# Routing in pairs, step-zero masks inside the last attention chunk, and low parts by ScalarE with accumulating transfers

## The chip, the cores and the metric

One core of one Trainium2 chip runs one program. The metric is device time in microseconds of one execution, the median of three. Before the change it is 358.88 us (358.85 to 359.8).

## What is computed

The input is x, 16 x 128 tokens of width 128, and a context of the same shape. Four residual layers follow; three start with a layer norm. The fourth is a routed feed-forward with two iterations, and its first lines are the router. From the reference, cut:

```python
x = x + _L0_xattn_ref(_layernorm(x), ctx, ctx, ...)
x = x + _L0_ffn_ref(_layernorm(x), ...)
x = x + _L1_xattn_ref(_layernorm(x), ctx, ctx, ...)
x = x + _L1_ffn_ref(_layernorm(x), ...)

# _L1_ffn_ref
logits = _gelu(xf @ w_r1 + b_r1) @ w_r2 + b_r2
top_p, top_i = jax.lax.top_k(softmax(logits), 2)       # of 8 experts
for _ in range(2):
    ctx = concat([integrated, v])
    shared_ctrl = _gelu(ctx @ w_s1 + b_s1) @ w_s2 + b_s2
    hidden = _gelu(einsum(ctx_e, expert_w1[flat_idx]) + b1)
    ctrl = einsum(hidden, expert_w2[flat_idx]) + b2     # alpha, beta, gate
    x_r, v_r = _inl(ctrl, x_e, v_e, mu)                 # softplus, sigmoid, combined by top_p
    halt = sigmoid(_gelu(x_next @ w_h1 + b_h1) @ w_h2 + b_h2)
    refined = _gelu(x_next @ w_f1 + b_f1) @ w_f2 + b_f2
    integrated = integrated + halt * refined * integration_weight
```

## The kernel before

The 2048 tokens are cut into four chunks of 512, each of four blocks of 128. The program of every engine is written out by hand; engines meet only at counted semaphores, and each executes its own list in order.

After the weights are composed comes a loop over slots t (0 to 5). In slot t the first feed-forward of chunk t, the attention of chunk t-1, the layer norm and router of chunk t-2 ("rt") and the routing of chunk t-3 are interleaved. A layer norm is `ln_tok` (TensorE turns tokens, L1276), `ln_stats` and `ln_scale` (VectorE, L788 to L803) with the power -1/2 by GpSimd between them (L359), and `ln_zt` (TensorE turns back, L1297). `busy` multiplies without using the result; the table `FILL` and slot 4 place 9 such matmuls ahead of the attention norm of chunk 2, 2 and 14 ahead of the router norms of chunks 2 and 3, and 7 ahead of an expansion. `route(c)` (L847 to L863) is a chain of 14 small VectorE operations that finds the two experts of the tokens; `expand(c)` and `expand_weights(c)` (L1371, L1383, eight small transposes each) spread expert numbers and factors over the partitions, and ScalarE evicts them (L452, L458); `weigh` computes the factors and `slot_masks` the bias masks.

The fourth layer is a loop over eight steps s: chunks 0 to 3 in iteration one (s 0 to 3) and again in iteration two (s 4 to 7). TensorE in step s does `hidden(s+1)` (five tiles of three or, in iteration two, six matmuls, into two PSUM banks in turn, so that tile 2 waits until ScalarE has evicted tile 0), then the parts `controls(s, BETA)`, ALPHA (iteration two alone) and GATE. All these are float32r products in three pieces, high*high, low*high and high*low. ScalarE applies softplus or tanh to a part (`squashed`) and gelu to hidden tiles (L482, L484). VectorE makes the masked copies: `kept(s, j)` for tiles j = 1 to 3 (L897, into the two buffers hm), then in `lower(s, j)` their high part (L913, a cast) and their low part (L915, a subtraction of what the cast kept):

```python
dve.tensor_copy(out[:, 0, i, :], hm[j % 2]).then_inc(sem("hhi"), 1)
dve.wait_ge(sem("hhi"), (HT - 1) * s + j)
dve.tensor_tensor(out[:, 1, i, :], hm[j % 2], out[:, 0, i, :].bitcast(F), ALU.subtract)\
    .then_inc(sem("hlo"), 1)
```

`stepped(s)` combines the parts on VectorE (L1109 and on), and `refine_a`, `halt_a`, `refine_b` with `refine1`, `halt1`, `refine2` are the halt and refinement of the step before. GpSimd issues four accumulating transfers xi onto xT (L365).

## Time and profile before

| | |
|---|---|
| median of the runs | 358.88 us |
| the profiled execution's own time | 360.02 us |
| its span, first to last instruction | 358.2 us |
| TensorE matmul busy | 327.9 us (92%) |
| VectorE busy | 284.2 us (79%) |
| ScalarE busy | 196.2 us (55%) |
| GpSimd busy | 21.1 us (6%) |
| mean granted TensorE clock | 0.981 |

The times and the rows below come from one profiled execution. "Idle before" is time in which an engine waited, with what ended it. "PEclk" is the granted TensorE clock as a share of full speed, 2.4 GHz; 0.50 is 1.2 GHz. Starts are in us from the span's start.

### The profile page before, as it was taken

Reading aid. Unit: us, or ns where it says so; the run is one execution under the profiler, and the core shown is the slowest. Engines: PE = TensorE matmul, PEld = TensorE weight load, DVE = VectorE, ACT = ScalarE, POOL = GpSimd, SP = SyncE. Lnnn points to the kernel's source line nnn. Section 1 sums busy time; section 2 is a strip of 40 time slices with the busy share of each in tenths; the row PEclk is TensorE's granted clock in tenths of the full one; section 3 lists DMA queues with packets and bytes.
Section 4 is the critical chain, followed back from the end, with each engine's and each line's share of the span. In section 5 each row is a group of like instructions: output and inputs, shape, how many; then the busy total and the mean of one; then the engine's idle time right before and its main releaser. Section 6 shows DMA issues by size and latency. Waiting matters only on the chain.

```text
span 358.2 us, 4385 instructions
## 1 busy us (share of the span) xinstructions
PE 327.9 (92%) x1513; PEld 231.5 (65%) x1521; DVE 284.2 (79%) x598; ACT 196.2 (55%) x309; POOL 21.1 (6%) x24
## 2 busy tenths in 40 slices
PE   4989999899888889599798999999999999999996
PEld 4754787445454557367476677777777777777663
DVE  0556767655768777979997999999997997999694
ACT  2500025385637285186876686775855846734744
POOL 0040020202010112000000100000000000000000
PEclk9989999999999999789899999999999999999999
DMA  7999920000000000000000010100100100000001
...
DMA packets 11445, 18.92 MB, mean 53 GB/s; under 512 B 416, under 2 KB 8864, under 8 KB 10144
## 3 DMA queue, kind: packets, MB, share of 16 engines
...
q0 software_dynamic: 576, 1.05, 1.7%
...
HBM read 16.55 MB, written 1.05 MB: 49 GB/s over the span
## 4 chain that ended last, share of the span: by engine, by line
PE 70%; DVE 19%; issue 4%; ACT 3%; POOL 3%; DMA 2%; SPq 0%; DVEq 0%; ACTq 0%; POOLq 0%
PE ps L1200 65%; DVE zz L803 4%; POOL lrs L359 3%; DVE lst L788 2%; DMA ctxT<-in_ctxT 2%; PE ps L1297 1%; PE ps L1383 1%; PE ps L1276 1%; DVE lmv L791 1%; DVE st L688 1%; ACT hid L484 1%; PE ps L1371 1%; DVE a L704 1%; DVE lve L793 1%; DVE ctxT L1090 0%
## 5 line engine op out<-in xcount | busy, mean ns | idle before, releaser
L1200 PE MATMUL ps<-hm_odd,ew_hi 128*128 128x512 f32 (+1 forms) x164 | 52.3, 421 | 0.0
L1200 PE MATMUL ps<-hm_even,ew_hi 128*128 128x512 f32 (+1 forms) x160 | 49.7, 414 | 0.0
L1200 PEld LDWEIGHTS ps<-hm_odd,ew_hi 128*128 128x128 f32 (+1 forms) x164 | 29.1, 191 | 6.5 <-issue 0.5
L1200 PEld LDWEIGHTS ps<-hm_even,ew_hi 128*128 128x128 f32 (+1 forms) x160 | 27.5, 188 | 5.2
L1200 PE MATMUL ps<-hm_odd,ew_lo 128*128 128x512 f32 (+1 forms) x80 | 28.8, 397 | 0.0
L1200 PE MATMUL ps<-hm_even,ew_lo 128*128 128x512 f32 (+1 forms) x80 | 28.0, 390 | 0.0
L484 ACT ACTIVATE hid<-ps,pB 128x512 f32<-128x512 f32 x32 | 21.7, 687 | 10.4 <-PE ps L1200 9.7
L1200 PE MATMUL ps<-x_hi,w1x_hi 128*128 128x512 f32 x40 | 20.1, 503 | 5.7 <-ACT hid L484 3.9
L803 DVE TENSOR_SCALAR zz<-ps,lmv,lrs 128x128 f32<-128x128 f32 x48 | 16.4, 405 | 7.7 <-POOL lrs L359 7.5
L897 DVE SCALAR_TENSOR_TENSOR ring<-ring,pB,hid 128x1024 f32<-128x1024 bf16 x16 | 20.5, 1283 | 0.9
L788 DVE BATCH_NORM_STATS2 lst<-ps 128x6 f32<-128x128 f32 x48 | 10.7, 285 | 11.9 <-PE ps L1276 11.8
L1200 PE MATMUL ps<-zz,pB 128*128 128x512 f32 (+3 forms) x52 | 19.5, 503 | 0.5 <-DVE zz L1133 0.5
L359 POOL TENSOR_TENSOR lrs<-lve,mhalf 128x4 f32<-128x4 f32 x12 | 13.1, 1089 | 107.2 <-DVE lve L793 107.2
L1200 PE MATMUL ps<-ring,a 128*128 128x512 f32 x32 | 16.0, 652 | 1.0 <-DVE a L704 1.0
L1200 PE MATMUL ps<-x_lo,w1x_hi 128*128 128x512 f32 x40 | 16.9, 423 | 0.0
L1200 PE MATMUL ps<-x_hi,w1x_lo 128*128 128x512 f32 x40 | 16.7, 417 | 0.0
L1200 PEld LDWEIGHTS ps<-hm_odd,ew_lo 128*128 128x128 f32 (+1 forms) x80 | 14.2, 191 | 3.0
L1200 PE MATMUL ps<-zz,wz 128*128 128x512 f32 x32 | 15.7, 596 | 0.0
L1200 PEld LDWEIGHTS ps<-hm_even,ew_lo 128*128 128x128 f32 (+1 forms) x80 | 13.7, 188 | 2.7
L595 ACT ACTIVATE kv<-ps 128x1024 f32<-128x1024 f32 x15 | 15.3, 1017 | 0.0
L1200 PEld LDWEIGHTS ps<-b,ring 128*128 128x128 f32 x128 | 14.7, 192 | 0.6 <-issue 0.5
L1200 PE MATMUL ps<-b,ring 128*128 128x128 f32 x128 | 15.0, 276 | 0.0
...
## 6 DMA issues: line engine op xcount, KB each, us to landing
...
```

What stands on the lines that cost most here:

```text
L359: pool.tensor_tensor(lrs[:, n % 2, :], lve[:, n % 2, :], mhalf[:, 0:BPC], ALU.pow)\
L484: act.activation(hid[:, j, :], hid_bank(s, j), ACT.Gelu, bias=W("eb1", j, j + 1)).then_inc(sem("hid"), 1)
L595: act.activation(out[:, 1:3], group_ps(n)[:, 1:3], f, scale=scale).then_inc(sem("squash"), 1)
L688: dve.bn_stats(st[:, b, :], xtok[:, b, :]).then_inc(sem("st"), 1)
L704: dve.tensor_tensor(a1[:, :, :], a1[:, :, :], wcol[:, 0, :].unsqueeze(2).to_broadcast([128, KC, D]), ALU.mult).then_inc(sem("a1s"), 1)
L788: dve.bn_stats(lst[:, n % 2, j, :], t[:, j * D:(j + 1) * D]).then_inc(sem("lst"), 1)
L791: dve.bn_aggr(lmv[:, n % 2, j, :], lst[:, n % 2, j, :]).then_inc(sem("lmv"), 1)
L793: dve.tensor_scalar(lve[:, n % 2, :], lmv[:, n % 2, :, 1], EPS, None, ALU.add)\
L803: dve.tensor_scalar(ztok[:, n % 2, j, :], t[:, j * D:(j + 1) * D], lmv[:, n % 2, j, 0:1], lrs[:, n % 2, j:j + 1], ALU.subtract, ALU.mult)\
L897: dve.scalar_tensor_tensor(hm[j % 2], idx[:, c, :, :], W("tile_expert", j, j + 1), hid[:, j, :].unsqueeze(1).to_broadcast([128, 2, CH]), A ...
L1200: return pe.matmul(out, lhsT, rhs, start=start, stop=stop)
L1276: last = pe.transpose(bank[n % 2][:, j * 128:(j + 1) * 128], xT[:, t * 128:(t + 1) * 128], ident)
```

## The change

Routing runs for two chunks at a time: `logits(c)` copies each chunk's logits alone, and `route(c)` and `weigh(c)` work on eight blocks. In slots 2 and 3 no routing, expansion or weighing is left between the norms. The slots end after t = 3; the rest of chunk 3's attention, the router norms of chunks 2 and 3 and the hidden tiles and masks of step 0 follow in a list of their own, in which the hidden tiles come in the order 1, 2, 0, 3 and shared. The 23 `busy` matmuls ahead of the router norms and the expansion are gone. `controls(0, BETA)` now stands ahead of `router2(3)` and `hidden(1)`, with the last router norm inside it; expansions and weights of later chunks move into steps 0, 1 and 2.

For tiles 2 and 3 of every step VectorE no longer subtracts. ScalarE writes the negated high part (`negative_high`; the target is float32r, so the copy rounds) into the low half of the masks, and GpSimd adds the unrounded masks by an accumulating transfer of 128 x 1024 (`low_part`), 16 in all. In a BETA part the high products of tiles 2 and 3 now come ahead of all their low products. Three PSUM banks swap roles with the other three, which changes no count.

```diff
-            for n in range(3 * NCH):
+            def power(n):
                 pool.wait_ge(sem("lve"), n + 1)
                 pool.tensor_tensor(lrs[:, n % 2, :], lve[:, n % 2, :], mhalf[:, 0:BPC], ALU.pow)\
...
-            for s in range(NCH):
+            def low_part(s, j):
+                pool.wait_ge(sem("nhi"), 2 * s + j - 1)
+                if s >= 1:
+                    pool.wait_ge(sem(f"hlo_{j}"), 16 * s)
+                pool.dma_start(low_of(s, j), hm[j % 2], accum_op=ALU.add).then_inc(sem(f"hlo_{j}"), 16)
...
+            for n in range(3 * NCH - 1):
+                power(n)
+            low_part(0, 2)
+            power(3 * NCH - 1)
+            low_part(0, 3)
+            for s in range(1, STEPS):
+                if 3 <= s < NCH + 3:
+                    residual(s - 3)
+                low_part(s, 2)
+                low_part(s, 3)
...
+            def negative_high(s, j):
+                act.wait_ge(sem("hm"), (HT - 1) * s + j)
+                act.activation(low_of(s, j), hm[j % 2], ACT.Copy, scale=-1.0).then_inc(sem("nhi"), 1)
+            z_att(3)
+            q_evac(3)
+            expand_evac(0, 2, 3)
+            exps(3)
+            second_exp(0)
+            hidden_gelus(0, (1, 2))
+            ln_evac("rt", 2, xi[:, ck(2)])
+            hidden_gelus(0, (0, 3))
+            r1_gelu(2)
+            hidden_gelus(0, (HT,))
+            negative_high(0, 2)
+            expand_evac(1, 3, 2)
+            ln_evac("rt", 3, xi[:, ck(3)])
+            negative_high(0, 3)
+            r1_gelu(3)
...
             for s in range(STEPS):
+                if s == 0:
+                    squashed(0, BETA)
+                    hidden_gelus(1)
+                    state_high(2)
+                    second_exp(2)
+                    weights_evac(0, 7, 6)
+                    expand_evac(2, 7, 6)
+                    negative_high(1, 2)
+                    negative_high(1, 3)
+                    squashed(0, GATE)
+                    continue
                 if s + 1 < STEPS:
                     hidden_gelus(s + 1)
-                if s == 0:
-                    second_exp(NCH - 2, 2)
                 if s == 1:
-                    weights_evac(NCH - 1, 7, 6)
+                    expand_evac(3, 7, 6)
+                    weights_evac(1, 7, 6)
                 if s >= 2:
                     refine2(s - 2)
+                if s == 2:
+                    weights_evac(2, 7, 6)
+                    weights_evac(3, 7, 6)
                 if s + 2 < STEPS:
                     state_high(s + 2)
                 squashed(s, BETA)
-                if s >= 1:
+                refine1(s - 1)
+                halt1(s - 1)
+                if s + 1 < STEPS:
+                    negative_high(s + 1, 2)
+                    negative_high(s + 1, 3)
                 squashed(s, parts(s)[1])
...
+            def logits(c):
+                t = slice(c * BPC, (c + 1) * BPC)
+                dve.wait_ge(sem("lg_ps"), c + 1)
+                dve.tensor_copy(lg[:, t, :], router_bank(c)[:, 0:BPC * E].rearrange("p (b e) -> p b e", b=BPC))\
+                    .then_inc(sem("lg"), 1)
...
+                t = slice(c * BPC, (c + 2) * BPC)
+                eq = eq_2[:, :, :]
+                iota = W("iota").unsqueeze(1).to_broadcast([128, 2 * BPC, E])
...
+            def high(s, j):
+                dve.wait_ge(sem("hm"), (HT - 1) * s + j)
+                dve.tensor_copy(high_of(s, j), hm[j % 2]).then_inc(sem("hhi"), 1)
...
                 kept(s, 2)
+                if s == 2:
+                    weigh(2)
                 if next_state:
                     state_split(s + 1)
                 lower(s, 0)
+                high(s, 1)
                 lower(s, 1)
                 kept(s, 3)
-                lower(s, 2)
+                high(s, 2)
                 shared_halves(s)
-                lower(s, 3)
+                high(s, 3)
+                if s <= 2:
+                    slot_masks(s + 1)
...
+            route(0)
+            att_add(2)
+            ln_stats("rt", 2)
+            att_max(3)
+            slot_masks(0)
+            ln_scale("rt", 2)
+            kept(0, 1)
+            att_norm(3)
+            high(0, 1)
+            lower(0, 1)
             kept(0, 2)
-            lower(0, 1)
+            att_pt(3)
+            high(0, 2)
+            att_add(3)
+            logits(2)
+            slot_masks(1)
+            ln_stats("rt", 3)
             kept(0, 3)
+            lower(0, 0)
+            ln_scale("rt", 3)
+            high(0, 3)
+            shared_halves(0)
             state_split(1)
-            lower(0, 2)
-            shared_halves(0)
-            lower(0, 3)
-            route(NCH - 1)
+            weigh(0)
+            logits(3)
+            route(2)
             dve.wait_ge(sem("consts"), 4)
...
-            FILL = {("att", 0): 5, ("att", 1): 4, ("att", 2): 9, ("rt", 2): 2, ("rt", 3): 14}
+            FILL = {("att", 0): 5, ("att", 1): 4, ("att", 2): 9}
...
+            att_v(2)
+            ln_zt("att", 3)
+            q_proj(3)
+            pe.wait_ge(sem("fh"), FT * NCH)
+            expand(0, 2, 3)
+            ln_tok("rt", 2, "x3")
+            scores(3)
+            hidden(0, (1, 2))
+            ln_zt("rt", 2)
+            hidden(0, (0, 3))
+            probs_t(3)
+            router1(2)
+            hidden(0, (HT,))
+            router2(2)
+            att_v(3)
+            pe.wait_ge(sem("hid"), HT)
+            pe.wait_ge(sem("hsu"), 1)
+            expand(1, 3, 2)
+            ln_tok("rt", 3, "x3")
             pe.wait_ge(sem("bp"), 1)
...
+                def high(i):
+                    j, k = TILES[i]
+                    pe.wait_ge(sem("hhi"), (HT - 1) * s + j)
+                    mm((lo, hi)[k], weights(ew2_hi, j), m[:, 0, i, :], start=rows_last and j == 1, stop=False)
+                    mm((lo, hi)[k], weights(ew2_lo, j), m[:, 0, i, :], start=False, stop=False)
+                def low(i):
+                    j, k = TILES[i]
+                    if j == 1:
+                        pe.wait_ge(sem("hlo"), 1 if s == 0 else 2 * s + 2)
+                    else:
+                        pe.wait_ge(sem(f"hlo_{j}"), 16 * (s + 1))
+                    last = mm((lo, hi)[k], weights(ew2_hi, j), m[:, 1, i, :], start=False,
+                              stop=not rows_last and j == HT - 1)
+                    if n == LAST and j == HT - 1:
+                        last.then_inc(sem("stream_ps"), 1)
+                    return last
...
                 for i in (1, 3, 5, 2, 4, 6) if n == LAST else range(1, NT):
-                    j, k = TILES[i]
-                    if i == 4 and between:
-                        between()
-                    pe.wait_ge(sem("hlo"), HT * s + j + 1)
-                    out = hi if k else lo
-                    mm(out, weights(ew2_hi, j), m[:, 0, i, :], start=rows_last and j == 1, stop=False)
-                    mm(out, weights(ew2_lo, j), m[:, 0, i, :], start=False, stop=False)
-                    last = mm(out, weights(ew2_hi, j), m[:, 1, i, :], start=False,
-                              stop=not rows_last and j == HT - 1)
-                    if n == LAST and j == HT - 1:
-                        last.then_inc(sem("stream_ps"), 1)
+                    if i in between:
+                        between[i]()
+                    high(i)
+                    if not rows_last or i < 3:
+                        last = low(i)
+                if rows_last:
+                    for i in range(3, NT):
+                        low(i)
                 if rows_last:
                     shared(True)
...
+                if s == 0:
+                    def routed():
+                        ln_zt("rt", 3)
+                        router1(3)
+                    def weights_0():
+                        pe.wait_ge(sem("hid"), 2 * HT)
+                        pe.wait_ge(sem("hsu"), 2)
+                        expand_weights(0, 7, 6)
+                    def expand_2():
+                        pe.wait_ge(sem("cb"), 2)
+                        expand(2, 7, 6)
+                    controls(0, BETA, between={5: routed})
+                    router2(3)
+                    hidden(1)
+                    controls(0, GATE, between={2: weights_0, 4: expand_2})
+                    continue
+                def expand_3():
+                    pe.wait_ge(sem("hid"), 3 * HT)
+                    pe.wait_ge(sem("hsu"), 3)
+                    expand(3, 7, 6)
+                def weights_1():
+                    pe.wait_ge(sem("idx"), 2 * NCH)
+                    expand_weights(1, 7, 6)
+                def weights_2():
+                    pe.wait_ge(sem("rr"), 1)
+                    pe.wait_ge(sem("th"), 1)
+                    expand_weights(2, 7, 6)
+                def weights_3():
+                    pe.wait_ge(sem("cb"), 6)
+                    expand_weights(3, 7, 6)
                 if s + 1 < STEPS:
                     hidden(s + 1)
                 if s >= 2:
                     refine_b(s - 2)
```

How it moves instructions at the three places that matter:

VectorE in slot 3, from the statistics of chunk 3's attention norm. Before (L788, L793 statistics, L847 to L863 routing, L803 scaling):

```order
180 L793 TENSOR_SCALAR lve<-lmv 128x4 [waits lmv]
181 L847 COPY lg<-ps 128x32 [waits lg_ps]
182 L850 TENSOR_REDUCE rt<-lg 128x4 [waits lg]
183 L851 TENSOR_TENSOR eq<-lg,rt 128x32 [waits dve_chain]
184 L852 TENSOR_TENSOR eq<-eq,pB 128x32 [waits dve_chain]
```

Now:

```order
156 L846 TENSOR_SCALAR lve<-lmv 128x4 [waits lmv]
157 L856 TENSOR_SCALAR zz<-ps,lmv,lrs 128x128 [waits zt_ps,lrs]
158 L856 TENSOR_SCALAR zz<-ps,lmv,lrs 128x128 x3
159 L895 COPY lg<-ps 128x32 [waits lg_ps]
160 L908 TENSOR_REDUCE rt<-lg 128x8 [waits lg]
161 L909 TENSOR_TENSOR eq<-lg,rt 128x64 [waits dve_chain]
```

The scaling stands ahead of the routing, which handles two chunks in one chain.

TensorE in the part BETA of step 0, tiles 1 and 2, before (each hlo is counted up by a subtraction on VectorE):

```order
220 L1200 MATMUL ps<-hm_even,ew_hi 128x512 [waits hlo]
221 L1200 MATMUL ps<-hm_even,ew_lo 128x512
222 L1200 MATMUL ps<-hm_even,ew_hi 128x512
223 L1200 MATMUL ps<-hm_even,ew_hi 128x512 [waits hlo]
224 L1200 MATMUL ps<-hm_even,ew_lo 128x512
225 L1200 MATMUL ps<-hm_even,ew_hi 128x512
```

Now, from the turning back of chunk 3's router norm (pA,zz) and `router1(3)` (xi,pB) in the middle of that part to its end; hlo_2 and hlo_3 are the semaphores of the transfers:

```order
190 L1365 MATMUL ps<-pA,zz 128x128 [waits ztok,z]
191 L1365 MATMUL ps<-pA,zz 128x128 x3
192 L1268 MATMUL ps<-xi,pB 32x512 [waits lg,x2,z]
193 L1268 MATMUL ps<-hm_even,ew_hi 128x512 [waits hhi]
194 L1268 MATMUL ps<-hm_even,ew_lo 128x512
195 L1268 MATMUL ps<-hm_even,ew_hi 128x512 [waits hhi]
196 L1268 MATMUL ps<-hm_even,ew_lo 128x512
197 L1268 MATMUL ps<-hm_even,ew_hi 128x512 [waits hlo_2] x2
198 L1268 MATMUL ps<-hm_even,ew_hi 128x512 [waits hlo_3] x2
199 L1268 MATMUL ps<-hsh,ws_hi 128x512 [waits hsl]
```

The last router norm and its transfer now lie inside a part, whose last products wait for tile 3's transfer.

ScalarE at the end of step 1, before (L565 and L566 are `halt1`, L594 and L595 the squashed GATE, L482 the next hidden tile 0):

```order
115 L565 ACTIVATE zz<-ps,pB 128x512 [waits h1_ps]
116 L566 ACTIVATE h1s<-ps,pB 128x512
117 L594 ACTIVATE kv<-ps,bs2h 128x512 [waits part_ps,xn]
118 L595 ACTIVATE kv<-ps 128x1024
119 L482 ACTIVATE hm_odd<-ps,pB 128x512 [waits part_ps,hlo,hid_ps]
```

Now:

```order
117 L608 ACTIVATE h1s<-ps,pB 128x512
118 L565 ACTIVATE hm_even<-wz 128x1024 [waits hm]
119 L565 ACTIVATE hm_even<-ring 128x1024 [waits hm]
120 L636 ACTIVATE kv<-ps,bs2h 128x512 [waits part_ps,xn]
121 L637 ACTIVATE kv<-ps 128x1024
122 L519 ACTIVATE hm_odd<-ps,pB 128x512 [waits part_ps,hlo,hid_ps]
```

The two negated copies stand between `halt1` and the squashed GATE.

## Rows read from the trace of the kernel before

**Rows 1.** Stretches, all engines: us, busy (count) per engine, PEclk, DMA share, GB/s

```profile
99.71:122.43 22.72, 19.17 (x100) 12.65 (x99) 17.26 (x74) 10.65 (x23) 2.06 (x3) 1.00 0.00 1
122.43:156.78 34.35, 26.72 (x125) 18.65 (x128) 27.49 (x84) 18.01 (x34) 2.99 (x2) 0.90 0.00 0
156.78:197.63 40.85, 36.84 (x173) 27.28 (x173) 36.77 (x50) 30.50 (x43) 0.00 (x0) 0.96 0.01 1
197.63:331.72 134.09, 134.09 (x599) 98.82 (x603) 125.81 (x135) 84.12 (x114) 3.65 (x4) 1.00 0.05 10
```

**Rows 2.** Timeline of TensorE, waits of 1 us and more, and the late one

```profile
150.31 0.99 PE L1200 MATMUL ps<-x_hi,w1x_hi 128*128 128x512 f32 x1 [1.60 <-DVE x_lo L929]
...
174.50 0.50 PE L1200 MATMUL ps<-x_hi,w1x_hi 128*128 128x512 f32 x1 [2.65 <-ACT hid L484]
...
195.89 0.50 PE L1200 MATMUL ps<-x_hi,w1x_hi 128*128 128x512 f32 x1 [1.28 <-ACT hid L484]
...
332.60 0.47 PE L1200 MATMUL ps<-xn_hi,wf_hi 128*128 128x512 f32 x1 [0.87 <-issue]
```

**Rows 3.** Stretches around two falls of the granted clock (PEclk third from the end)

```profile
150.31:155.00 4.69, 4.57 (x10) 3.08 (x11) 4.49 (x8) 1.92 (x3) 0.00 (x0) 0.50 0.00 0
172.40:175.80 3.40, 1.30 (x6) 1.05 (x6) 3.33 (x3) 2.91 (x5) 0.00 (x0) 0.99 0.00 0
175.90:179.10 3.20, 3.20 (x9) 2.28 (x8) 3.13 (x4) 2.15 (x4) 0.00 (x0) 0.50 0.01 3
```

**Rows 4.** Timeline of VectorE: one of each kind of its work

```profile
98.80 0.19 DVE L850 TENSOR_REDUCE rt<-lg 128x4 f32<-128x32 f32 x1
...
116.76 0.89 DVE L788 BATCH_NORM_STATS2 lst<-ps 128x6 f32<-128x128 f32 x4 [0.95 <-PE ps L1276]
...
118.05 0.18 DVE L847 COPY lg<-ps 128x32 f32<-128x32 f32 x1
...
120.92 1.37 DVE L803 TENSOR_SCALAR zz<-ps,lmv,lrs 128x128 f32<-128x128 f32 x4
122.20 0.74 DVE L835 SCALAR_TENSOR_TENSOR xT<-ps,bvo,xT 128x512 f32<-128x512 f32 x1
...
144.29 1.28 DVE L897 SCALAR_TENSOR_TENSOR wz<-ring,pB,hid 128x1024 f32<-128x1024 bf16 x1
145.49 0.69 DVE L913 CAST hm_even<-ring 128x1024 fp32r<-128x1024 f32 x1
146.21 1.23 DVE L915 TENSOR_TENSOR hm_even<-ring,hm_even 128x1024 fp32r<-128x1024 f32 x1
```

**Rows 5.** Groups of the small transposes, 99 to 200 us: busy, mean ns | idle before

```profile
L1371 PE MATMUL ps<-pA,tif 128*128 128x128 f32 x32 | 4.3, 276 | 0.9 <-DVE tif L862 0.9
L1383 PE MATMUL ps<-pA,cf 128*128 128x128 f32 x32 | 4.2, 275 | 0.0
```

**Rows 6.** Timeline of ScalarE: a copy, a table load, two ends of step, hidden tile 0

```profile
159.67 0.62 ACT L547 ACTIVATE x_hi<-xi 128x512 fp32r<-128x512 f32 x1
...
160.92 1.28 ACT L594 ACT_TABLE_LOAD   x1
...
193.08 0.69 ACT L594 ACTIVATE kv<-ps,bs2h 128x512 f32<-128x512 f32 x1 [0.90 <-PE ps L1200]
193.66 1.02 ACT L595 ACTIVATE kv<-ps 128x1024 f32<-128x1024 f32 x1
...
214.06 0.69 ACT L594 ACTIVATE kv<-ps,bs2h 128x512 f32<-128x512 f32 x1 [0.88 <-PE ps L1200]
214.65 1.02 ACT L595 ACTIVATE kv<-ps 128x1024 f32<-128x1024 f32 x1
...
216.21 1.50 ACT L484 ACTIVATE hid<-ps,pB 128x512 f32<-128x512 f32 x2
```

**Rows 7.** Timeline of TensorE, tile 2 of `hidden(4)`, next to rows 6

```profile
216.95 0.50 PE L1200 MATMUL ps<-x_hi,w1x_hi 128*128 128x512 f32 x1
```

**Rows 8.** The accumulating transfers: L365's landing, and the queue (packets, MB, share)

```profile
DMA to landing us min/median/max: 3.3/3.4/3.7
...
q0 software_dynamic: 576, 1.05, 1.7%
```

More of the change, by code:

```diff
@@ L513, in _ @@
                     q_evac(t - 1)
-                if f and t:
+                if t:
                     gelus(t, (3,))
@@ L1003, in _ @@
             weights_low()
-            for t in range(SLOTS):
-                f, a, q, x = (0 <= t - i < NCH for i in range(4))
+            for t in range(NCH):
+                a, q = t >= 1, t >= 2
                 if t + 2 < NCH:
@@ L1011, in _ @@
                     ln_scale("ffn", t + 2)
-                if x and not f:
-                    slot_masks(t - 3)
                 if q:
                     ln_stats("rt", t - 2)
-                if t == SLOTS - 1:
-                    kept(0, 1)
-                    lower(0, 0)
                 if a:
```

270 lines of the change are left out of this document (106 added, 164 removed).

## Prediction

> **What bounds the kernel now.** I read the stretches first. From 197.63 to 331.72 us TensorE is busy for the whole 134.09 us, at full clock, while VectorE is busy for 125.81 and ScalarE for 84.12 [rows 1]. So in steps 2 to 7 only TensorE's own work counts, one matmul per 0.22 us (134.09 / 599). Ahead of that it is not full: 19.17 of 22.72, 26.72 of 34.35 and 36.84 of 40.85 us, part of it at a lowered clock. The timeline says why [rows 2]: it waits 1.60 us for VectorE's x_lo, and 2.65 and 1.28 us for ScalarE's hidden tile 0. The 0.87 us at 332.60 is again a wait for VectorE (the second input split of step 6), although the row says issue. The reader should see that the change can gain only ahead of 197.63 us and at that late wait, and lose anywhere.
>
> **The sum** goes along the path that leads to the first step without waits, against the profiled execution's own span of 358.2 us (its own time is 360.02, 1.1 above the median 358.88; I add the difference to the median). "Lead" is how much earlier a thing happens than before.
>
> *To the last attention norm.* In slot 3 the routing of 14 small operations stands between statistics and scaling: from 118.05 to 120.92 us, 2.9 us [rows 4]. It moves behind; the power on GpSimd, about 1 us, stays. That gives some 1.7 us, and the same in the slot before gives 1.3, since TensorE's nine filling matmuls then end last. One expansion and one set of weights leave the slot, 1.07 us each (4.3 us for four) [rows 5]. Lead 1.7 + 1.3 + 2.1 = 5.1: the scaled tokens of chunk 3's attention are complete at 117.2 instead of 122.3.
>
> *To the last router norm.* Now VectorE has the whole list to itself, and TensorE waits for it; the 23 fills that go had filled such waits (5.2 us), so they give nothing, but they had held the clock up. By kinds [rows 4]: two statistics 2.8 with their aggregates, two scalings 2.6, three masked copies at 1.2 make 3.6, two casts 1.4, low parts 1.25 and 0.65, two additions 1.4, two pairs of bias masks 1.4, attention maximum, norm and copy 2.3, logits 0.2. The paired routing is 14 operations at 0.22 us on twice the columns. Its bounds are 2.9 (no more than one chunk now) and 5.7 (twice that); I take 3.1, as the 0.19 us of these tiny tiles [rows 4] is mostly fixed. Sum 20.7. Waits between them: 0.8 for token transposes, 1.7 for ScalarE (four exponentials, a table load of 1.28 [rows 6], one gelu), 0.5 and 0.6 for the attention output and the expansion. 24.2 in all: the last router norm is scaled at 141.4; before it was ready at 144.4, ahead of the row at 144.29 [rows 4]. The lead is down to 3.
>
> *Into the first part.* BETA of step 0 has begun at 135.6 by the same addition, but needs tile 3's low part: transposes 0.5, eviction 0.6, the negated copy, then the transfer. The copy is bounded by two of the 0.62 us copies and by the 1.02 us of a 1024-wide eviction [rows 6]; I take 1.0. The transfer moves 512 KB; the trace shows 256 KB landing in 3.3 to 3.7 us [rows 8]. Bounds are 3.4 (size costs nothing) and 6.8 (all of it scales). The queue's share, 1.7% of 16 engines' span, is 97 us for 576 packets, so 0.17 each; 128 over 16 engines take 1.35 us, doubling adds that: 4.75, which I take. The Trainium skill, DMA: Bandwidth & Descriptors, section Anatomy of one DMA, gives 2.0 us plus bytes over 436e3 instead, an estimate of 3.2 us; by that the sum would end 1.5 us lower. The rows, with 3.4 for half the size, speak for more. So 143.5 + 4.75 = 148.2.
> The rest of the part is 1.85 us. TensorE will have waited about 3.3 us twice; before, after a stretch with 1.30 of 3.40 us busy, 3.2 us at half clock followed [rows 3], so I add 1.5: 151.6. ScalarE then squashes (1.6), loads gelu (1.3) and makes tile 0 (1.3) before TensorE's last three tiles of `hidden(1)` (2.2): 158.0. GATE with 2.0 us of transposes takes 7.6 and ends at 165.6. Before, that was 174.50 - 2.65 - 1.75 = 170.1 [rows 2].
>
> *Steps 1 to 3.* In step 0 ScalarE has x_hi, a load, weights and expansion (to 164.3), two negated copies, GATE (1.6), a load, and tile 0: `hidden(2)` goes on at 170.5 instead of 174.5. Lead 4.0. BETA of step 1 holds one expansion more; I count 0.6 of its 1.0, as a half-clock stretch of before [rows 3] becomes shorter: 3.4. At the end of a step ScalarE used to wait 0.90 and 0.88 us for TensorE ahead of GATE [rows 6]. Now two copies, 2.0 us, stand there, so GATE is 1.1 late, and with it the next tile 0, for which TensorE already waits at 195.89 [rows 2]: 2.3. Step 2 gets the weights of chunks 2 and 3, which used to be done by then, in the full stretch: -2.1, left 0.2. At the ends of steps 2 and 3 the two copies cost again. Tile 2 of `hidden(4)` starts at 216.95 [rows 7], when the gelus that began at 216.21 have just made tile 0 [rows 6], so nearly nothing hides them: 2 x 1.05 = 2.1. In steps 4 to 6 the copies stand ahead of ALPHA and the GATE part hides them; if it didn't, three more such microseconds would come. VectorE has 2.5 us less per step (two times 1.23 [rows 4]), so the late wait of 0.87 goes; ScalarE's chain is next there. At the end of step 1 TensorE waits 2.5 us, which may lower the clock: 0.8.
> In all 3.4 - 1.1 - 2.1 - 2.1 + 0.9 - 0.8 = -1.8. **Forecast: 358.9 + 1.8 = 360.7 us**, own range 358.7 to 362.9 (transfer 3.4 or 6.8, clock lowered or not). About 0.3% (1.1 us) is what a measurement of this kernel can tell from no change.
>
> **Rivals.**
> *The lead survives (0.22).* For it: VectorE's list is shorter by 1.23 us twice a step, and every TensorE wait ahead of 197.63 has VectorE or ScalarE as its end. If the low part lands in 3.4 us (1.35 less) and the clock stays up (1.5 and 0.8 less), the sum is 1.8 - 3.7 = -1.9: 357.0 us. It decides whether TensorE reaches step 2 more than 4.5 us ahead, which pays for the late weights and the copies. Against: without the fills TensorE is emptier than in the stretch that lost its clock [rows 3].
> *Late low parts (0.17).* One GpSimd queue carries 20 transfers instead of four. If a 512 KB one needs 6.8 us or more, TensorE stands 2 us longer in BETA of step 0, and at 8 us 3.3: 362.7 to 364. In later steps the masks are made 10 us ahead, so only this one counts. The four landings, 3.3 to 3.7 us beside running VectorE work [rows 8], speak against it. The Trainium skill, SBUF — State Buffer, section on the two separate sides, says that a VectorE copy between SBUF tiles in its fast mode keeps GpSimd from writing descriptors, so such a transfer seems blocked. Here each transfer of tile 3 is issued next to a cast of 0.69 us [rows 4]; as a mechanism of this kernel that adds up to 0.7 us and gives 361.4, inside my own range.
> *VectorE was the pace (0.02).* It is 94% busy in the full stretch [rows 1]. If it set the step, 2.46 us in each of six steps would go: 344 us. TensorE's 134.09 us without a gap speak against it.
> *It does nothing on balance (0.04):* the moved work was hidden anyway, 358.9.
>
> **Chances.** Forecast 0.55, of which 0.21 lies within 0.3%; the lead survives 0.22, mostly over 0.3% faster; late low parts 0.17; the rest 0.06. Faster 0.21, same 0.25, slower 0.54. The range for 8 in 10 reaches to the first rival and to the second: 356.7 to 364.7.
>
> **What would show it.** The scaled tokens of chunk 3's attention near 117; TensorE waiting 3 us and more in BETA of step 0 for a transfer issued near 143.5; landings of 4.5 to 5 us; `hidden(3)` tile 2 near 193.5 after a wait of 2.5 us; new waits of about 1 us ahead of tile 2 in `hidden(4)` and `hidden(5)`; none for x_lo near 332. The prediction is wrong if TensorE has no waits at the ends of steps 2 and 3, if the negated copies take well under 1 us, or if the full stretch starts more than 4 us earlier.

## The result, and the profile after

| | before | changed |
|---|---|---|
| median of the runs | 359.34 us (358.85 to 359.83, 4 runs) | 365.35 us (363.7 to 366.37, 4 runs) |
| ratio, 95% interval | | 1.0163 (1.0119 to 1.0207) |
| span of the profiled execution | 358.2 us | 364.2 us |
| mean granted TensorE clock | 0.981 | 0.963 |
| TensorE, VectorE busy | 327.9, 284.2 us | 328.4, 259.6 us |
| ScalarE, GpSimd busy | 196.2, 21.1 us | 210.6, 35.2 us |

The changed kernel is 6.0 us slower. The forecast had the sign, with 1.8 us, but 365.35 lies above the range's end of 364.7. VectorE was relieved by 24.6 us, and the kernel still became longer. The changed kernel's profile is that of its slowest run, 366.37 us.

The same four stretches as in [rows 1], changed kernel:

```profile
99.71:122.43 22.72, 19.10 (x86) 11.64 (x85) 14.89 (x55) 9.72 (x20) 2.43 (x3) 0.93 0.00 1
122.43:156.78 34.35, 25.20 (x110) 16.03 (x108) 20.04 (x55) 17.21 (x32) 4.98 (x4) 0.80 0.16 31
156.78:197.63 40.85, 33.58 (x166) 24.50 (x165) 32.78 (x58) 34.19 (x49) 3.77 (x4) 1.00 0.18 34
197.63:331.72 134.09, 132.11 (x589) 97.54 (x590) 110.41 (x120) 93.39 (x128) 12.04 (x14) 0.99 0.29 55
```

The second stretch stands out: the granted clock is 0.80 where it was 0.90, although TensorE has less to do. VectorE is busy for only 20.04 of its 34.35 us, so its own work doesn't fill the stretch; what it waits for is read below.

TensorE's timeline of the changed kernel, its waits and what ran behind them ([rows 2, 7] for before):

```profile
117.72 0.63 PE L1365 MATMUL ps<-pA,zz 128*128 128x128 f32 x4 [1.72 <-DVE zz L856]
119.09 1.87 PE L1268 MATMUL ps<-wz,pB 128*128 128x512 f32 x2 [0.75 <-ACT wz L435]
...
127.41 0.63 PE L1365 MATMUL ps<-pA,zz 128*128 128x128 f32 x4 [1.90 <-DVE zz L856]
...
133.71 1.92 PE L1268 MATMUL ps<-xi,pB 128*32 128x512 f32 x2
...
146.48 0.94 PE L1365 MATMUL ps<-pA,zz 128*128 128x128 f32 x4 [3.70 <-DVE zz L856]
148.11 1.91 PE L1268 MATMUL ps<-xi,pB 128*32 128x512 f32 x2 [0.69 <-ACT xi L435]
...
153.93 0.73 PE L1268 MATMUL ps<-hm_even,ew_hi 128*128 128x512 f32 x2 [1.05 <-DMA hm_even<-ring]
...
172.43 0.38 PE L1268 MATMUL ps<-xtok,others 128*128 128x512 bf16 x1 [1.75 <-DVE xtok L943]
...
175.33 0.50 PE L1268 MATMUL ps<-x_hi,w1x_hi 128*128 128x512 f32 x1 [1.13 <-ACT hid L521]
...
198.04 0.80 PE L1268 MATMUL ps<-x_hi,w1x_hi 128*128 128x512 f32 x1 [2.17 <-ACT hid L521]
...
223.13 0.51 PE L1268 MATMUL ps<-x_hi,w1x_hi 128*128 128x512 f32 x1 [0.80 <-ACT hid L521]
...
246.90 0.50 PE L1268 MATMUL ps<-x_hi,w1x_hi 128*128 128x512 f32 x1 [0.77 <-ACT hid L521]
```

The clock can be read from the second number, the duration. The projection at 119.09 and the router products at 133.71 and 148.11 take 1.87 to 1.92 us; at the full clock they take 1.04 to 1.12, as kernel e1 below shows. The clock has fallen three times by 150 us, each time behind waits. The wait at 172.43 is new, for chunk 2's slot masks; those at 223.13 and 246.90, ahead of tile 2 of `hidden(4)` and `hidden(5)`, are new too and were forecast (about 1 us each). VectorE's waits for TensorE behind the first and the second low stretch, and the queue and landings (min, median, max) of the transfers:

```profile
123.25 0.89 DVE L841 BATCH_NORM_STATS2 lst<-ps 128x6 f32<-128x128 f32 x4 [1.79 <-PE ps L1344]
...
139.02 0.75 DVE L888 SCALAR_TENSOR_TENSOR xT<-ps,bvo,xT 128x512 f32<-128x512 f32 x1 [3.76 <-PE ps L1268]
...
DMA to landing us min/median/max: 4.6/4.8/6.5
...
q0 software_dynamic: 2880, 9.44, 13.9%
```

### The profile page after: what moved, and what is told of

Same layout as the page of the kernel before. It is cut to its first block, busy times and chain, and to the rows that moved or that the text cites. A ratio compares the mean times of both kernels' runs of the same rounds, so it can differ in the third digit from the quotient of the medians.

```text
span 364.2 us, 4348 instructions
## 1 busy us (share of the span) xinstructions
PE 328.4 (90%) x1498; PEld 228.5 (63%) x1498; DVE 259.6 (71%) x546; ACT 210.6 (58%) x324; POOL 35.2 (10%) x40
## 3 DMA queue, kind: packets, MB, share of 16 engines
HBM read 16.55 MB, written 1.05 MB: 48 GB/s over the span
## 4 chain that ended last, share of the span: by engine, by line
PE 66%; DVE 13%; ACT 8%; issue 5%; POOL 3%; DMA 3%; SPq 0%; DVEq 0%; ACTq 0%; POOLq 0%
PE ps L1268 61%; DVE zz L856 3%; POOL lrs L378 3%; DVE lst L841 2%; PE ps L1365 2%; DMA ctxT<-in_ctxT 2%; ACT hid L521 1%; DMA hm_even<-ring 1%; PE ps L1344 1%; PE ps L1439 1%; PE ps L1449 1%; DVE st L741 1%; DVE lmv L844 1%; ACT zz L607 1%; ACT kv L636 1%
## 5 line engine op out<-in xcount | busy, mean ns | idle before, releaser
L1268 PE MATMUL ps<-hm_even,ew_hi 128*128 128x512 f32 (+1 forms) x160 | 51.8, 425 | 1.1 <-DMA hm_even<-ring 1.1
L959 DVE SCALAR_TENSOR_TENSOR ring<-ring,pB,hid 128x1024 f32<-128x1024 bf16 x16 | 20.5, 1283 | 3.3 <-ACT hid L521 1.6
L1268 PE MATMUL ps<-ring,a 128*128 128x512 f32 x32 | 17.3, 696 | 1.0 <-DVE a L757 1.0
L1365 PE MATMUL ps<-pA,zz 128*128 128x128 f32 x48 | 7.9, 288 | 11.2 <-DVE zz L856 11.2
L1268 PEld LDWEIGHTS ps<-x_hi,w1x_hi 128*128 128x128 f32 x40 | 8.1, 203 | 15.0 <-ACT hid L521 12.4
L1365 PEld LDWEIGHTS ps<-pA,zz 128*128 128x128 f32 x48 | 5.3, 143 | 17.1 <-issue 15.0
```

What stands on the lines that cost most here:

```text
L959: dve.scalar_tensor_tensor(hm[j % 2], idx[:, c, :, :], W("tile_expert", j, j + 1), hid[:, j, :].unsqueeze(1).to_broadcast([128, 2, CH]), A ...
L1268: return pe.matmul(out, lhsT, rhs, start=start, stop=stop)
L1365: last = pe.transpose(bank[6][:, j * 128:(j + 1) * 128], ztok[:, n % 2, j, :], ident)
```

## The experiments

Executions differ by up to 1.6 us already at the first norm's transposes (47.17 to 48.76 us), up to which all these kernels do the same work. The table counts from there, in us. Each row is one profiled execution, whose own time is given ("profiled"); it isn't always near the median, so differences below 1 or 2 us between ends are not to be read from it. The kernel before was run beside each of these kernels, with medians of 359.25 to 359.48. Below, brackets behind a time hold the lowest and highest run, those behind a ratio its 95% interval.

| kernel | chunk 3's last norm, transposes | hidden(2), first gelu | hidden(3), first gelu | end | profiled | median us |
|---|---|---|---|---|---|---|
| before | 96.6 | 125.3 | 146.7 | 310.4 | 360.02 | 359.3 |
| changed | 98.3 | 125.8 | 148.5 | 316.0 | 366.37 | 365.35 |
| e1: fills | 94.5 | 123.2 | 145.9 | 312.1 | 363.02 | 363.76 |
| e2: before without fills | 98.5 | 127.0 | 148.1 | 311.8 | 361.31 | 361.29 |
| e3: copies behind the gate | 98.2 | 127.4 | 152.3 | 322.9 | 373.62 | 372.56 |
| e4: all lows on VectorE | 97.2 | 127.6 | 150.2 | 315.8 | 365.49 | 365.78 |
| e11: step 0's lows on VectorE | 97.9 | 125.4 | 148.0 | 314.3 | 363.8 | 364.13 |
| e6: fills, masks, step 0's lows | 94.5 | 119.4 | 142.8 | 309.1 | 359.27 | 357.05 |
| e7: fills, masks, lows of steps 0 to 4 | 94.4 | 117.8 | 143.3 | 308.2 | 357.65 | 358.2 |
| e9: e7 and chunk 3's masks | 94.4 | 117.8 | 139.6 | 304.8 | 353.81 | 354.14 |
| e10: e9, all lows on VectorE | 94.4 | 117.8 | 139.6 | 305.5 | 354.53 | 355.42 |
| e12: e9 without fills | 98.2 | 125.6 | 147.4 | 312.3 | 362.83 | 362.38 |

**1. Fills back (e1).** `ew2_hi` products into a free bank, at three waits.

```diff
-            FILL = {("att", 0): 5, ("att", 1): 4, ("att", 2): 9}
+            FILL = {("att", 0): 5, ("att", 1): 4, ("att", 2): 9, ("att", 3): 7, ("rt", 2): 8, ("rt", 3): 14}
```

> The changed kernel with 29 filling matmuls put back into three waits of TensorE ahead of step 0: 7 ahead of the transposes of chunk 3's attention norm (1.72 us idle), 8 ahead of chunk 2's last norm (1.90 us) and 14 ahead of chunk 3's last norm (3.70 us); nothing else differs. Theory 1 (the forecast failed because TensorE ran at the lower clock in 119-122.5, 129-136 and 147-154 us, and that stretched the chain between VectorE and TensorE): the granted clock of 122-157 us rises from 0.80 to above 0.9, chunk 3's last norm is scaled at about 142 us in place of 144.97, step 0's Beta products end near 152 in place of 156, and the kernel takes 3 to 5 us less than the changed one's 365.35, so about 361. Theory 2 (the chain's length is set by VectorE, ScalarE and the transfer, and the lower clock only filled waits): under 1 us, so 364.5 to 366.

Measured: 363.76 us (362.58 to 364.51), ratio to before 1.0123 (1.0104 to 1.0142): 1.6 us less than the changed kernel. TensorE's timeline:

```profile
118.18 0.66 PE L1365 MATMUL ps<-pA,zz 128*128 128x128 f32 x4
119.59 1.12 PE L1268 MATMUL ps<-wz,pB 128*128 128x512 f32 x2 [0.75 <-ACT wz L435]
...
139.50 3.33 PE L1268 MATMUL ps<-ew_hi 128*128 128x512 f32 x14
143.25 0.66 PE L1365 MATMUL ps<-pA,zz 128*128 128x128 f32 x4 [0.42 <-DVE zz L856]
144.59 1.04 PE L1268 MATMUL ps<-xi,pB 128*32 128x512 f32 x2 [0.69 <-ACT xi L435]
...
150.41 0.98 PE L1268 MATMUL ps<-hm_even,ew_hi 128*128 128x512 f32 x2 [3.20 <-DMA hm_even<-ring]
151.20 0.63 PE L1268 MATMUL ps<-hsh,ws_hi 128*128 128x512 f32 x1
```

Its VectorE, at the two waits for TensorE that were shown for the changed kernel:

```profile
122.83 0.89 DVE L841 BATCH_NORM_STATS2 lst<-ps 128x6 f32<-128x128 f32 x4 [0.82 <-PE ps L1344]
...
135.87 0.75 DVE L888 SCALAR_TENSOR_TENSOR xT<-ps,bvo,xT 128x512 f32<-128x512 f32 x1 [1.03 <-PE ps L1268]
```

The clock stays up to 150 us (0.95 over 122 to 157 us, where the changed kernel had 0.80), and the last norm comes 3.8 us earlier (94.5 against 98.3). VectorE waits 0.82 us for the tokens in place of 1.79, and 1.03 us for the attention product in place of 3.76: 3.7 us together. At hidden(3) 2.6 us of it are left, and between the medians 1.6, though the intervals of the two kernels overlap. The rest is lost at the next limit: TensorE now waits 3.20 us for the transfer of tile 3's low part, and behind that wait the clock falls (0.63 us for one product, not 0.39). The expected size was wrong; the mechanism of theory 1 is there, with a second limit behind it.

**2. The kernel before without its 23 fills (e2).**

```diff
-            FILL = {("att", 0): 5, ("att", 1): 4, ("att", 2): 9, ("rt", 2): 2, ("rt", 3): 14}
+            FILL = {("att", 0): 5, ("att", 1): 4, ("att", 2): 9}
...
-                    busy(7 if t == SLOTS - 2 else 0, bank[2])
+                    busy(0, bank[2])
```

> The kernel before without its 23 filling matmuls in the two last slots (2 and 14 ahead of the last two norms, 7 ahead of an expansion). Theory 1 (these hold up the clock through the chain ahead of step 0): the stretch at 0.5 moves ahead of 147 us, the list is longer, and the kernel takes 2 to 4 us more than 359. Theory 2 (they only fill waits; the clock falls at 149.5 us with them anyway): within 1 us of 359.

Measured: 361.29 us (360.25 to 362.6), ratio 1.0060 (1.0039 to 1.0081). Stretches of the kernel before, then of this one:

```profile
143.00:150.00 7.00, 2.81 (x14) 1.57 (x14) 6.81 (x11) 1.28 (x2) 0.00 (x0) 0.89 0.00 0
```

```profile
143.00:150.00 7.00, 3.00 (x6) 0.90 (x6) 6.56 (x10) 0.64 (x2) 1.68 (x1) 0.64 0.00 0
```

The clock falls earlier, and the kernel takes 2.0 us more, at the lower end of theory 1's range. So dropping the fills with nothing else touched costs about two of the 6.0 us by which the changed kernel is slower.

**3. Negated copies behind the gate (e3).**

```diff
-                    negative_high(s + 1, 2)
-                    negative_high(s + 1, 3)
                 squashed(s, parts(s)[1])
+                if s + 1 < STEPS:
+                    negative_high(s + 1, 2)
+                    negative_high(s + 1, 3)
```

(and likewise in step 0)

> The changed kernel with ScalarE's two negated copies put behind the squashing of the step's last gate in steps 0 to 6, in place of ahead of it. Theory 1 (two copies of 0.94 us stand in the way of the squashing and of the next gelus at the ends of steps 1, 2 and 3, as the prediction has it at 1.1 and 1.05 each): 2.5 to 3.5 us less than the changed kernel, 362 to 363; the waits of TensorE at the next step's third hidden tile go back to those of before. Theory 2 (the copies then stand ahead of the next gelus and the low parts land too late for the next Beta products, so it is only moved): no change, 365, or slower.

Measured: 372.56 us (370.38 to 373.72), ratio 1.0366 (1.0340 to 1.0392): 7.2 us more than the changed kernel, a clear miss of theory 1. ScalarE at the end of step 1, first in the changed kernel, then in this one:

```profile
192.77 0.68 ACT L608 ACTIVATE h1s<-ps,pB 128x512 fp32r<-128x512 f32 x1
193.34 1.06 ACT L565 ACTIVATE hm_even<-wz 128x1024 fp32r<-128x1024 f32 x1
194.28 1.06 ACT L565 ACTIVATE hm_even<-ring 128x1024 fp32r<-128x1024 f32 x1
195.23 0.69 ACT L636 ACTIVATE kv<-ps,bs2h 128x512 f32<-128x512 f32 x1
...
196.71 0.70 ACT L519 ACTIVATE hm_odd<-ps,pB 128x512 fp32r<-128x512 f32 x1
```

```profile
195.96 0.68 ACT L608 ACTIVATE h1s<-ps,pB 128x512 fp32r<-128x512 f32 x1
197.53 0.69 ACT L636 ACTIVATE kv<-ps,bs2h 128x512 f32<-128x512 f32 x1 [0.89 <-PE ps L1268]
...
199.02 1.06 ACT L565 ACTIVATE hm_even<-wz 128x1024 fp32r<-128x1024 f32 x1
199.97 1.06 ACT L565 ACTIVATE hm_even<-ring 128x1024 fp32r<-128x1024 f32 x1
200.92 0.69 ACT L519 ACTIVATE hm_odd<-ps,pB 128x512 fp32r<-128x512 f32 x1
```

Ahead of the gate the copies stand partly in a wait of 0.89 us, so 1.9 us of copies cost about 1. Behind it they cost the whole 1.9 to the next gelus (from h1s to tile 0's first gelu 4.96 us, against 3.94). TensorE's wait at the third hidden tile is then 3.17 us in place of 2.17, with a half-clock stretch of over 4 us behind it. The place that the change chose was the better one.

**4. All low parts back on VectorE (e4).** `negative_high` and `low_part` do nothing, and in `high`:

```diff
+                if j >= 2:
+                    dve.wait_ge(sem("hhi"), (HT - 1) * s + j)
+                    dve.tensor_tensor(low_of(s, j), hm[j % 2], high_of(s, j).bitcast(F), ALU.subtract)\
+                        .then_inc(sem(f"hlo_{j}"), 16)
```

> The changed kernel with all low parts back on VectorE: no negated copies on ScalarE, no accumulating transfers; VectorE has two subtractions of 1.23 us more in each step and in the list ahead of step 0. Routing in pairs, the order of the list and the missing fills stay. Theory 1 (the prediction's: the copies cost 1.1 + 1.05 + 1.05 at ends of steps, the transfer's 4.6 us against 1.2 of a subtraction costs 2 to 3 ahead of step 0, the late low parts 0.9): 3 to 6 us less than the changed kernel, 359.5 to 362. Theory 2 (VectorE, which has two subtractions more ahead of the last norm and in each step, sets the pace): no better, 365 or more. If the fills alone explain the miss, this kernel still lies at or over 359.

Measured: 365.78 us (362.42 to 367.06), ratio 1.0164 (1.0128 to 1.0200): no better, the number of theory 2. In the trace the gain of theory 1 is there, `hidden(3)` to `hidden(4)` takes 22.96 us in place of 25.09 (23.82 in e1, with the clock up), but 1.7 us are lost ahead of that. This is TensorE's timeline:

```profile
173.61 0.99 PE L1268 MATMUL ps<-x_hi,w1x_hi 128*128 128x512 f32 x1 [4.10 <-DVE xtok L939]
```

The last operation of VectorE's list in a step is the pair of slot masks for the step after, which TensorE needs first. With two subtractions more ahead of it, the wait is 4.10 us, not 1.75. So it is less the pace of VectorE over a whole step than the place of the masks in its list. That led to the kernels e7 and e9.

**5. Slot masks early, with fills (e5).** In `hidden_masked`, besides the line of e1:

```diff
+                if s == 1:
+                    slot_masks(2)
                 high(s, 2)
                 shared_halves(s)
                 high(s, 3)
-                if s <= 2:
-                    slot_masks(s + 1)
+                if s == 2:
+                    slot_masks(3)
```

> The changed kernel with the 29 filling matmuls in three waits (363.76 us so) and with chunk 2's slot masks made before the cast of step 1's second tile, not after its last cast, so some 2 us earlier; TensorE waited 1.76 us for them ahead of the third step's hidden products. Theory 1 (that wait costs what it reads): 1.2 to 1.7 us less than 363.76. Theory 2 (ScalarE is still busy with the squashed gate and the gelu table load until the hidden products are there, and TensorE only meets it one tile later): within 0.4 us of 363.76, and TensorE's wait at the third hidden tile grows from 1.12 to above 2 us.

Measured: 363.99 us, ratio 1.0133 (1.0116 to 1.0149), so nothing against e1's 363.76: theory 2. e5 has no trace of its own that could be read. In e6, which has this edit and one more, the wait at the third hidden tile is 3.00 us at 169.09 in place of e1's 1.12; that fits the forecast growth, but isn't shown for e5 itself. The 1.75 us wait of the changed kernel is real in the trace and costs nothing by this run; there ScalarE loads its gelu table until 174.0, 1.6 us after TensorE's wait has ended.

**6. Step 0's low parts on VectorE, with fills and early masks (e6), and alone (e11).**

```diff
+                if j >= 2 and s < 1:
+                    dve.wait_ge(sem("hhi"), (HT - 1) * s + j)
+                    dve.tensor_tensor(low_of(s, j), hm[j % 2], high_of(s, j).bitcast(F), ALU.subtract)\
+                        .then_inc(sem(f"vlo_{j}"), 1)
```

(the negated copy and the transfer return early for `s < 1`)

> As the kernel with fills and early slot masks, and the low parts of step 0's tiles 2 and 3 by VectorE (two subtractions of 1.23 us) in place of negated copy and accumulating transfer; steps 1 to 7 keep the transfers. Theory 1 (with the clock restored, TensorE's 3.20 us wait for the transfer of tile 3's low part sets the end of step 0's Beta products): that wait goes, VectorE's list grows by up to 1.2 us ahead of chunk 3's last norm, and 2 to 2.8 us less, near 361.5. Theory 2 (VectorE's list is the pace, and the longer list takes back what the transfer gave): within 0.7 us of the same kernel with the transfers.

> The changed kernel with the low parts of step 0's tiles 2 and 3 by VectorE, and nothing else: no fills, masks where they were. With fills this edit took 6.9 us off together with the masks. Theory 1 (without the fills the clock falls and the late norm hides the transfer: TensorE waited only 1.05 us for it): 1 to 2 us less than 365.35, so the two repairs work only together. Theory 2 (the transfer's 4.6 us is a cost by itself): 4 to 6 us less, 359.5 to 361.5.

Measured: e6 357.05 us (356.54 to 359.27), ratio 0.9940 (0.9912 to 0.9969); e11 364.13 us (363.8 to 365.05), ratio 1.0144 (1.0125 to 1.0163). TensorE's timeline of e6, where e1 has its wait of 3.20 us:

```profile
142.86 0.66 PE L1378 MATMUL ps<-pA,zz 128*128 128x128 f32 x4 [0.30 <-DVE zz L860]
...
146.21 1.07 PE L1281 MATMUL ps<-hm_even,ew_hi 128*128 128x512 f32 x4
147.12 0.39 PE L1281 MATMUL ps<-hsh,ws_hi 128*128 128x512 f32 x1
```

Alone the edit gives 1.2 us by the medians, alone the fills give 1.6; together, with the masks, 8.3. The intervals of e11 and e1 overlap with that of the changed kernel, so each single gain may be anything from nothing to some 3 us; that their sum stays below 8.3 is beyond the noise. The masks were worth nothing in e5. In e6 they weren't taken out alone, but its trace leaves room: VectorE's last cast ends at 166.1, so masks made last would come 1.8 us after TensorE's start at 164.34, and ScalarE can't take tile 0 before 167.77 anyway. Each of the two costs had hidden the other: with late tokens the transfer was nearly covered (TensorE waited 1.05 us for it), and with the transfer the early tokens ran into a wait of 3.20 us, behind which the clock fell. In e6 two more subtractions on VectorE don't delay the last norm at all (94.5 in both).

**7. Low parts of steps 0 to 4 on VectorE (e7), chunk 3's masks early too (e9), all on VectorE (e10).** The limits `s < 1` become `s < 5` and `s < 8`; e9 and e10 have

```diff
-                high(s, 2)
-                shared_halves(s)
-                high(s, 3)
                 if s <= 2:
                     slot_masks(s + 1)
+                high(s, 2)
+                shared_halves(s)
+                high(s, 3)
```

> As the kernel before it, and the low parts of steps 0 to 4 by VectorE; only steps 5 to 7 keep the negated copies and transfers. Theory 1 (two copies of 0.94 us ahead of the squashed gate cost 0.9, 0.87 and 0.81 at the ends of steps 1, 2 and 3; in steps 4 to 7 TensorE has no waits, so they cost nothing there): 1.7 to 2.6 us less than with only step 0 on VectorE, near 359.3. Theory 2 (VectorE with 2.46 us more in each step gets late for the step's last products, as in the kernel before, and nothing is won): within 0.7 us.

> The kernel with 29 fills and the low parts of steps 0 to 4 on VectorE, and now chunk 3's slot masks too before the cast of step 2's second tile, some 5 us earlier; there TensorE waited 3.51 us for them ahead of hidden(3), and ScalarE 3.50 for TensorE. Theory 1 (this late pair of masks took the gain that the freed ScalarE had given): both waits go, ScalarE's gelus of hidden(3) start right behind the squashed gate, and 2.4 to 3.4 us less than 358.2, so 355 to 356. Theory 2 (VectorE's longer list delays the next step anyway): within 0.7 us of 358.2.

> As the kernel before it with all low parts on VectorE, so without negated copies and accumulating transfers in steps 5 to 7. Theory 1 (the transfers relieve VectorE near the end: from hidden(7)'s first gelu to the end it took 61.3 us with them and 62.2 without): 0.7 to 1.1 us more than the kernel before it. Theory 2 (TensorE is busy without a gap there, and who makes the low parts is nothing to it): the same within 0.3 us.

Measured: e7 358.2 us (357.03 to 360.33), ratio 0.9977 (0.9959 to 0.9995); e9 **354.14 us** (353.81 to 355.9), ratio **0.9865** (0.9845 to 0.9885); e10 355.42 us (354.53 to 356.88), ratio 0.9898 (0.9876 to 0.9920). TensorE at `hidden(3)`, e7 and then e9:

```profile
189.19 0.80 PE L1281 MATMUL ps<-x_hi,w1x_hi 128*128 128x512 f32 x1 [3.51 <-DVE xtok L947]
```

```profile
188.20 0.50 PE L1279 MATMUL ps<-x_hi,w1x_hi 128*128 128x512 f32 x1 [1.28 <-ACT hid L523]
```

ScalarE at the same place in e7, and TensorE near the end of e10 (e9 has no wait there):

```profile
190.88 0.69 ACT L521 ACTIVATE hm_odd<-ps,pB 128x512 fp32r<-128x512 f32 x1 [3.50 <-PE ps L1281]
```

```profile
327.07 0.47 PE L1279 MATMUL ps<-xn_hi,wf_hi 128*128 128x512 f32 x1 [0.86 <-issue]
```

e7 missed both ways: it was no faster than e6, but 1.1 us slower by the medians (the intervals overlap), and its longer list put the masks 3.51 us late. In e9 that wait is gone and 4.1 us with it, more than the row said, for the half-clock stretch behind it goes too. So the same kind of wait was worth nothing in e5 and 4.1 us here; what differs is ScalarE, which in e7 had nothing to do and waited 3.50 us for the hidden products. From e6 to e9 hidden(3) to hidden(4) falls from 23.84 to 23.14 us and hidden(4) to hidden(5) from 23.77 to 23.03: 0.7 each for two negated copies. And e10 against e9: without the transfers of steps 5 to 7 the late wait of the kernel before is back (0.86 us at 327.07), and from hidden(7)'s first gelu to the end it takes 62.18 us, not 61.38. So the transfers do help there, by 0.8 us in the traces and 1.3 between the medians.

**8. Ten more fills than e7, in three waits of 0.7 to 1.1 us (e8).** In `q_proj`, `hidden(0)` and `router1`:

```diff
+                if c == 3:
+                    busy(3, bank[5])
...
+                        if j == 0:
+                            pe.wait_ge(sem("x2"), NCH)
+                            pe.wait_ge(sem("lg"), 2)
+                            busy(4, bank[4])
...
+                if c == 3:
+                    busy(3, bank[1])
```

> As the kernel before it, with 10 more filling matmuls in three short waits of TensorE (3 while chunk 3's attention norm is evicted, 4 ahead of hidden tile 0, 3 while chunk 3's last norm is evicted). Theory 1 (short gaps one after the other bring the clock down too): the clock of 117 to 157 us is 1.00 throughout, and 0.5 to 1.5 us less. Theory 2 (only the three long waits mattered): the same time within 0.4 us.

Measured: 358.08 us (356.74 to 359.77), ratio 0.9974 (0.9955 to 0.9993); e7 was 358.2. Theory 2: with the three long waits filled, 122 to 157 us was at 1.00 already.

**9. The fastest kernel without the fills (e12).**

```diff
-            FILL = {("att", 0): 5, ("att", 1): 4, ("att", 2): 9, ("att", 3): 7, ("rt", 2): 8, ("rt", 3): 14}
+            FILL = {("att", 0): 5, ("att", 1): 4, ("att", 2): 9}
```

> The fastest kernel so far (354.14 us: fills, early slot masks, low parts of steps 0 to 4 on VectorE) with the 29 filling matmuls taken out again. Theory 1 (the fills are half of what the miss was: with the transfer gone from the list ahead of step 0, the clock is what is left there): the clock of 122 to 157 us falls to about 0.8, step 0's Beta products are evicted 3 to 5 us later, and 3 to 5 us more, 357 to 359. Theory 2 (the fills are worth no more than the 1.6 us that they gave the changed kernel, whatever else is there): 355.3 to 356.2.

Measured: 362.38 us (361.79 to 362.83), ratio 1.0084 (1.0070 to 1.0098): 8.2 us more than e9, beyond both theories; the mechanism is theory 1's, its size is double. Stretches of e9, then of e12:

```profile
129.00:136.00 7.00, 6.92 (x42) 5.02 (x43) 6.33 (x9) 5.13 (x9) 0.00 (x0) 1.00 0.01 2
...
143.00:150.00 7.00, 6.99 (x35) 4.71 (x35) 4.96 (x19) 4.96 (x6) 0.00 (x0) 1.00 0.00 0
150.00:157.00 7.00, 5.15 (x26) 3.37 (x26) 4.42 (x12) 6.12 (x10) 0.00 (x0) 1.00 0.00 0
157.00:164.00 7.00, 6.75 (x38) 5.19 (x35) 6.73 (x10) 4.76 (x9) 0.00 (x0) 1.00 0.01 2
```

```profile
129.00:136.00 7.00, 5.69 (x13) 2.58 (x14) 6.57 (x9) 3.31 (x6) 0.00 (x0) 0.57 0.00 0
...
143.00:150.00 7.00, 2.68 (x8) 0.71 (x6) 6.54 (x14) 0.60 (x1) 1.98 (x1) 0.79 0.00 0
150.00:157.00 7.00, 7.00 (x30) 5.25 (x31) 2.34 (x12) 3.98 (x5) 0.00 (x0) 0.72 0.00 0
157.00:164.00 7.00, 5.24 (x18) 3.27 (x18) 4.75 (x15) 5.39 (x9) 0.00 (x0) 0.77 0.00 0
```

Without fills TensorE is at half clock four times up to 164 us. Counted as in the table the norm is 3.8 us later, hidden(2) 7.7 and the end 7.6, so half of the loss comes behind the norm. These 29 products of 0.22 us each compute nothing, and without them this kernel too is slower than the one before.

## Why the prediction was off, step by step

- **To the last attention norm: right.** The scaling of its tokens ends at 117.6; forecast 117.2.
- **To the last router norm: this step failed.** The forecast let 24.2 us pass on VectorE from one scaling to the other (its own terms, 20.7 and 3.6, give 24.3), and took 3 us of lead out of it. The changed kernel took 28.8, and the scaling ended at 146.3 us, 1.9 behind before's 144.4 in place of 3.0 ahead. The work was right: 20.5 us for 20.7, and in it the paired routing 3.2 for 3.1. The term that failed is the waits between, put at 3.6 us; they measured 8.2, of which 3.76 are the wait at 139.02 where 0.5 was forecast. Behind it stands the sentence that the 23 fills "give nothing, but they had held the clock up": the forecast charged the lost clock to BETA alone (1.5 us), but VectorE's waits inside the list are for TensorE's products, and these ran at half clock. With fills (e1) the waits are 4.5 us and the list takes 25.1, 0.9 more than forecast. So of the 4.9 us of lead that were missing at the norm, 3.7 are the clock's; most of the rest is that 0.9.
- **Into BETA of step 0: right in its sum, not in its parts.** The copy takes 0.95 us (forecast 1.0), the transfer 4.6 to its landing (forecast 4.75, from rows 8). The Trainium skill, DMA: Bandwidth & Descriptors, section Anatomy of one DMA, would make it 3.2 by estimate; the measured 4.6, and 6.2 for the second of two issued together, decide against that here. But TensorE waited 1.05 us for it, not the forecast 3.3, since its products at half clock (148 to 153 us) filled the rest; the forecast had the half clock behind that wait. From the last norm to hidden(2)'s tile 2 the forecast had 29.1 us, and it took 29.0; to hidden(3)'s tile 2, 52.1 and 51.7. That the sums agree so well is in part luck: in e1, where wait (3.20) and clock lie as forecast, the first of them is 30.1.
- **Steps 1 to 3: nearly right.** The waits of about 1 us ahead of tile 2 in `hidden(4)` and `hidden(5)` came (0.80 and 0.77). hidden(3) to hidden(4) takes 25.09 us in place of 21.06: +4.0. Forecast were 2.1 for two weights, 1.05 for copies and 0.8 for the clock, 3.95; e1, in which the clock stays up there, has 23.82, so the clock's share was 1.3. hidden(4) to hidden(5) is 0.8 longer (1.05 forecast). The price of the copies was somewhat too high: by e6 and e9 it is 0.7 a step.
- **The late wait: right.** From hidden(7)'s first gelu to the end it takes 61.24 us in place of 62.17, 0.9 less.

In sum, counted as the forecast counts, from the span's start, 4.4 us of lead are missing at hidden(3) (2.1 us late in place of 2.3 early), and all that follows adds 3.9 where 4.1 was forecast.

The clock in the list isn't the whole miss, though. The fills alone (e1) bring the median down by 1.6 us only and leave it 4.4 above the kernel before. e1's own trace, counted as in the table, ends 1.8 us behind that of the kernel before (312.14 against 310.35), which is the forecast's number; what lies between that and its median is a start that was 0.9 us later, 0.3 us outside the span, and the distance of the two profiled runs from their medians (0.7 each).

Of the rivals, the one in which the lead survives needed a landing in 3.4 us and a clock that stays up; the landing took 4.6, and the clock fell, as its "against" had it. Even with the clock up to 150 us (e1) the lead at hidden(3) was 0.9 us, not enough. Late low parts were not what made the time long in the changed kernel (1.05 us of wait; e11, 1.2 us between medians), though e1 and e6 show what the transfer in step 0 costs once nothing else is late. VectorE wasn't the pace: it was relieved by 24.6 us and the kernel grew. The Trainium skill's rule on VectorE copies that hold up GpSimd's descriptors, in SBUF — State Buffer, section on the two separate sides, is borne out by no run here, nor excluded: none of them takes the casts away from beside the transfers.

What stays open: why the clock falls behind a wait in one execution and not in another with the same wait. Behind 1.72 and 0.75 us (117.72 and 119.09 in the changed kernel) it fell also in e3, e11 and e12 (1.83 to 2.07 us for the same two products), but not in e4 (1.13), whose list is the same up to there. Behind the wait of 1.76 us ahead of `hidden(1)`'s tile 2 it fell in e6 (0.63 us for a product at 154.08) and not in e7 (0.39 at 153.01). Behind 2.17 us at hidden(3) it fell in the changed kernel and not in e1. The changed kernel's spread, 363.7 to 366.37 us, goes with the mean clock of each run (0.976 to 0.963).

## What to carry to other kernels

Before you take work out of an engine that "only fills a wait", look at which chain it keeps short: here the price of the missing fillers was not only TensorE's own products at half clock, but also every wait of VectorE for such a product. Two costs in a row on one chain can hide one another, so single repairs (1.6 and 1.2 us) can look poor when the pair is worth 8.3; try them together before you drop either. And before you count a wait in a timeline at its length, look at the engine that needs the waiting one's result: where ScalarE was busy, the late masks cost nothing, and where it waited, the same pair of masks of 0.72 us at the end of VectorE's list cost 4.1. Put first in an engine's list what the next stage starts with.

## What the runs showed that had not been expected

- The clock fell behind waits as short as 1.72 and 0.75 us with 0.63 us of work between them (117.72 and 119.09 in the changed kernel), while in e9, with waits of 0.75, 0.59 and 1.10 us left and the longer ones filled, it was still at 1.00 from 117 us on, and two later waits of 1.76 and 2.64 us did not bring it down.
- The value of 29 filling products depends on what else is on the chain: 1.6 us with the transfer in the way, 8.2 without. The 23 of the kernel before were worth 2.0.
- Two accumulating transfers of 512 KB issued 0.9 us apart land 4.6 and 6.2 us after their issue; GpSimd is occupied for 0.86 us by each.
- A run's time is longer than its span by 2.1 to 2.2 us in the changed kernel, e1, e3 and e5, which issue all 20 accumulating transfers, and by 1.8 us in all others, which issue 18 (e6) or fewer. No run here shows why.
